# First-step keys loaded whole in the middle, the middle's last stores moved into the attention, filling products ahead of the first 42 half maxima

## What is computed

```python
# layer 0: state space model, then a feed-forward with signs for weights
u  = ssm(layernorm(x))                         # a scan over 2048 steps
y  = clip(layernorm(x) @ sign(W).T * scale + bias)
x1 = x + u + y;  xn = layernorm(x1)
# layer 1, two attentions, 16 heads of 16 features, causal
A  = softmax(q @ k.T / 4 + slope * (j - i)) @ v     # from xn, 16 key heads
B  = softmax(rope(q) @ rope(k).T / 4) @ v           # from rmsnorm(xn), 4 key heads
# then output products, a router, and the two best of 8 experts for each token
```

## Time and profile before

| | us |
|---|---|
| median of three runs | 2366.09 (2365.41 to 2367.84) |
| the profiled execution, its own time | 2358.44 |
| its span, first to last instruction | 2356.0 |
| TensorE busy | 2176.4 (92%) |
| VectorE busy | 2028.9 (86%) |
| ScalarE busy | 1542.3 (65%) |
| GpSimd busy | 671.4 (28%) |
| mean granted clock of TensorE | 0.956 of 2.4 GHz |

### The profile page before, as it was taken

One profiled execution on the slowest core, in us unless ns is written; L12 is line 12 of the kernel. 1 busy time (PEld: TensorE's weight loads), 2 busy tenths in 40 slices (PEclk: granted clock), 3 DMA queues, 4 the chain that ended last, 5 costly groups with the idle time before them and its releaser, 6 DMA issues. The chain is left out here.

```text
span 2356.0 us, 47793 instructions
## 1 busy us (share of the span) xinstructions
PE 2176.4 (92%) x15828; PEld 1282.4 (54%) x15829; DVE 2028.9 (86%) x5148; ACT 1542.3 (65%) x2993; POOL 671.4 (28%) x997
## 2 busy tenths in 40 slices
PE   4599968999999999999999999999998894999997
PEld 2355544444444444444444544544543783888886
DVE  7799858999999999999999999999991664777775
ACT  3144414678888888888888888888888452444443
POOL 5523002232322322322322322322211254333333
PEclk8799977999999999999999999999999886999999
DMA  5179875654554654432432432433222895444443
GB/s 169 58 217 266 276 179 77 119 118 90 103 107 88 108 107 86 92 84 63 92 85 63 92 78 70 92 76 72 69 89 64 292 307 215 78 81 81 82 81 70
DMA packets 176412, 273.23 MB, mean 116 GB/s; under 512 B 53608, under 2 KB 126072, under 8 KB 170372
## 3 DMA queue, kind: packets, MB, share of 16 engines
q0 software_dynamic: 45840, 137.55, 28.6%
q1 hardware_dynamic: 125332, 122.86, 17.3%
q10 hardware_dynamic: 5044, 10.32, 1.5%
HBM read 128.64 MB, written 140.98 MB: 114 GB/s over the span
## 5 line engine op out<-in xcount | busy, mean ns | idle before, releaser
L1524 ACT ACTIVATE a_p<-banks 128x512 f32<-128x512 f32 x2176 | 1131.2, 608 | 256.8 <-PE banks L1417 206.8
L1577 DVE TENSOR_REDUCE a_mx<-banks 128x1 f32<-128x512 f32 x1536 | 943.4, 680 | 20.1 <-PE banks L1406 20.0
L1485 PE MATMUL banks<-a_p,a_v 128*32 128x512 f32 (+3 forms) x5120 | 589.0, 544 | 1.6 <-ACT a_o L1542 1.1
L1406 PE MATMUL banks<-a_k,a_q 52*128 52x512 f32 (+5 forms) x1600 | 446.8, 413 | 1.9 <-DVE a_rowtop L1574 0.3
L1417 PE MATMUL banks<-a_q,a_k 50*128 50x512 f32 (+7 forms) x1600 | 415.8, 396 | 1.1
L1574 DVE CUSTOM_DVE_ANT_0 a_masked<-banks,a_later 128x512 bf16<-128x512 f32 (+3 forms) x768 | 330.8, 484 | 19.2 <-PE banks L1406 17.3
L1417 PEld LDWEIGHTS banks<-a_q,a_k 54*128 54x128 f32 (+1 forms) x1600 | 227.3, 185 | 198.7 <-DVE a_mx L1577 95.6
L1406 PEld LDWEIGHTS banks<-a_k,a_q 52*128 52x128 f32 (+1 forms) x1600 | 224.1, 185 | 118.0 <-DVE a_mx L1577 55.4
L1406 PE MATMUL banks<-a_k,q 48*128 48x512 f32 (+6 forms) x896 | 256.7, 420 | 6.2 <-DMA a_k<-aug_rows 4.6
L1417 PE MATMUL banks<-q,a_k 50*128 50x512 f32 (+7 forms) x896 | 231.5, 402 | 1.1 <-DVE a_orow L1597 0.3
L1485 PEld LDWEIGHTS banks<-a_p,a_v 128*32 128x32 f32 x5120 | 109.3, 108 | 175.0 <-issue 125.3
(11 more groups left out here) (276 smaller groups left out, 2997.2 us busy)
## 6 DMA issues: line engine op xcount, KB each, us to landing
expert_rows<-a_zeros POOLq DMA_DIRECT2D x132, 258.0 KB, 5.3
a_k<-ka_parts POOLq DMA_DIRECT2D x42, 256.0 KB, 6.3
e_x<-expert_rows SPq DMA_DIRECT2D x71, 129.0 KB, 2.3
expert_rows<-e_y SPq DMA_DIRECT2D x71, 128.0 KB
qa_parts<-m_part SPq DMA_DIRECT2D x16, 512.0 KB
ka_parts<-m_part SPq DMA_DIRECT2D x16, 512.0 KB
va_tiles<-m_va SPq DMA_DIRECT2D x8, 1024.0 KB, 6.8
qb_parts<-m_part SPq DMA_DIRECT2D x16, 512.0 KB, 3.8
```

Source lines behind the costliest of these rows:

```text
L1406: ins = pe.matmul(ps[bank][:, col:col + w], q_op[r % 3][part, p, qt * P:(qt + 1) * P], keys_of(r, k0)[part, kp, k0:k0 + w], start=True, st ...
L1485: ins = pe.matmul(ps_o[VW * h:VW * h + VW, c0:c0 + w], v_op[o][:, kt, hk * VW:hk * VW + VW], prob[:, (at + slot) % NPB, col:col + w], star ...
L1524: nc.scalar.activation(prob[:, (t * NSC + n) % NPB, :], ps[bank][:, :], ACT.Exp, scale=SCALE).then_inc(s_ex, 1)
L1577: ins = v.tensor_reduce(top, ps[bank][:, :], AX.X, ALU.max)
```

## The change

- `k0a` (keys of 512 tokens) is gone. `k0`, all 2048 keys of step 0, 16 KB a partition, lies where the first half of `xnT` (the normalised tokens of batch 0) lay, which nobody reads after block 3. POOL loads it in the middle in three groups, the first with the extras, after block 6's second low part, block 6's last, and block 7's second. `first_step_keys`, `keys_of` and the waits on `s_k` are gone.
- The stores of the last `kb` part and of the last `vb` tile are issued by SP first thing in the attention; SP awaits no part or value store at the middle's end, and POOL awaits all of them ahead of the first load of step 1 after half maximum 40.
- `later` and `numbers` are loaded in the front; all engines wait for `s_masks` 80.
- Filling products: 36 instead of 20 at the middle's end; none ahead of the first rows instead of 10; two ahead of each of the first 17 half maxima (`ROWLESS` = 7 + 2 * 5 = 17) and one ahead of each of the next 25 (`WARM` = 42), into the bank just taken.
- Tiles of the attention are allocated in another order.

```diff
             for dst, src in ((M["fill"], "c_fill"),
+                             (M["later"], "c_later"), (M["numbers"], "c_ids"),
...
-def first_keys(eng, M, j):
-    for n in range(NPROD):
...
+def first_keys(eng, M, j, n):
+    at = HALF * j + n * HD
+    eng.dma_start(M["k0"][at:at + HD, :, :].bitcast(F32),
+                  M["ka_d"][PROD_K[n], 0:GH * HD, :].rearrange("(p j d) t -> j d p t", p=PAIRS, j=2)[j]
+                  ).then_inc(M["s_first"], 16)
+
+def first_operands_at(nc, M):
+    at = SBUF_START + F32_BYTES * (P + WIDE + TOK // P + PAIRS * L) + BF16_BYTES * (HALF + 2 * P)
+    M["k0"] = nc.alloc_sbuf_tensor_at("k0", [P, PAIRS, L], F32R, offset=at)
...
+def last_stores(eng, M):
+    eng.dma_start(M["kb_d"][:, (B - 1) * P:B * P, L - BT:L].rearrange("a f t -> f a t"),
+                  M["last_part"][:, :, :].bitcast(F32)).then_inc(M["s_moved"][NBLK - 2], 16)
+    eng.dma_start(M["vb_d"].rearrange("(n p) c -> p n c", p=P)[:, TOK // P - TPB:TOK // P, :],
+                  M["last_values"][:, :, :, :].rearrange("p j h c -> p j (h c)")).then_inc(M["s_moved"][NBLK - 1], 16)
...
@@ middle, POOL @@
-                    for m in range(2):
+                    for m in range(4):
                         pool.wait_ge(s_pst[m], NBB * 16 + 16)
...
-            for j in range(2):
-                first_extras(pool, M, j)
-                first_keys(pool, M, j)
+            for n, rows in enumerate(((NBLK - 2) * NS + 2, (NBLK - 2) * NS + NS, (NBLK - 1) * NS + 2)):
+                pool.wait_ge(s_lo, rows)
+                for j in range(2):
+                    first_keys(pool, M, j, n)
+                    if n == 0:
+                        first_extras(pool, M, j)
...
@@ middle, SP @@
                     sp.wait_ge(s_lo, blk * NS + (m + 1))
+                    if blk == NBLK - 1 and m == NS - 1:
+                        break
...
                 sp.wait_ge(s_va, blk * 2 + 2)
-                sp.dma_start(vb_d[:, blk * TPB:(blk + 1) * TPB, :],
-                             vb[:, :, :, :].rearrange("p j h c -> p j (h c)")).then_inc(s_vst, 16)
-            for m in range(NS):
-                sp.wait_ge(s_pst[m], NBLK * 16 + 16)
+                if blk < NBLK - 1:
+                    sp.dma_start(vb_d[:, blk * TPB:(blk + 1) * TPB, :],
+                                 vb[:, :, :, :].rearrange("p j h c -> p j (h c)")).then_inc(s_vst, 16)
             for i in range(2):
                 sp.wait_ge(s_st[i], NBLK // 2 * 32 + 16)
-            sp.wait_ge(s_vst, NBLK * 32 + 16)
             sp.wait_ge(M["s_first"], NFIRST)
...
-            keep_going(pe, M, ps[0], 20)
+            keep_going(pe, M, ps[0], 36)
...
@@ attention, SP @@
+            last_stores(sp, M)
             for o in range(2):
                 sp.sem_inc(s_os[o], 16)
-            sp.dma_start(later[:, :], A["c_later"]).then_inc(M["s_masks"], 16)
-            first_step_keys(sp, s_k[0], BT, 2 * BT)
...
@@ attention, POOL @@
-            pool.dma_start(numbers[:, :], A["c_ids"]).then_inc(s_zs, 16)
             pool.wait_ge(s_hi, 1)
-            pool.wait_ge(s_zs, 16)
+            pool.wait_ge(M["s_masks"], NMASKS)
...
                     elif t == 0 and what == "max" and n % 5 == 0 and 0 <= n // 5 - 4 < len(LOADS):
+                        if n // 5 == 4:
+                            for done, count in zip(M["s_moved"], M["moved"]):
+                                pool.wait_ge(done, count)
                         pool.wait_ge(s_mt, 2 * n)
                         load(pool, 1, LOADS[n // 5 - 4])
...
@@ attention, PE @@
-                        if t == 0 and n == 2 * KEYED[0]:
-                            pe.wait_ge(s_k[0], NFK)
-                        if t == 0 and n == 2 * KEYED[1]:
-                            pe.wait_ge(s_k[1], NFK)
...
                         take(bank, s_md, t * NMH + (n + 1 + MD0))
+                        if t == 0 and n < WARM:
+                            keep_going(pe, M, ps[bank], 2 if n < ROWLESS else 1)
                         max_half(t + n // NMH, n, bank)
                     elif what == "rows":
-                        if t == 0 and n == 0:
-                            keep_going(pe, M, ps_o, 10)
...
@@ attention, ACT @@
-            first_step_keys(act, s_k[1], 2 * BT, L)
             load(act, 0, ("values", 0, 0))
```

More of the change, by code:

```diff
@@ L13 @@
 ds = bass.ds
+SBUF_START, SBUF_END = 16512, 229344
+F32_BYTES, BF16_BYTES = 4, 2
 P = 128
@@ L156, in _ @@
             sp.dma_start(aug[:, :], A["c_aug"]).then_inc(s_aug, 16)
-            for dst, src in ((M["fill"], "c_fill"),
+            for dst, src in ((M["fill"], "c_fill"), (M["later"], "c_later"), (M["numbers"], "c_ids"),
                              (M["after_q"][0], "c_after0"), (M["after_q"][1], "c_after1")):
@@ L514, in middle @@
         vb_d = M["vb_d"].rearrange("(n p) c -> p n c", p=P)
+        M["last_part"], M["last_values"] = part[NS - 1], vb
         NW = 10
@@ L1105, in attention @@
         ps, ident = M["ps"], M["ident"]
-        q_op = [M["q0"], *(sb(f"a_q{i}", [P, PAIRS, L], F32R) for i in range(1, 3))]
+        sb("a_room_k0", [P, PAIRS, L], F32R)
+        q1 = sb("a_q1", [P, PAIRS, L], F32R)
         v_op = [sb(f"a_v{i}", [P, KT, GH * VW]) for i in range(3)]
@@ L1109, in attention @@
         fill, after_q = M["fill"], M["after_q"]
-        later = sb("a_later", [P, WIDE])
+        later, numbers = M["later"], M["numbers"]
         masked = sb("a_masked", [P, 2, WIDE], BF16)
@@ L1119, in attention @@
         zeros = sb("a_zeros", [P, FILL, DR])
-        numbers = sb("a_numbers", [P, TOK // P])
         raw_w = sb("a_raww", [P, WIDE], F32R)
         high_w = sb("a_highw", [P, WIDE], F32R)
-        k_op = [sb(f"a_k{i}", [P, PAIRS, L], F32R) for i in (0, 2, 1)]
-        k_op = [k_op[0], k_op[2], k_op[1]]
+        q_op = [M["q0"], q1, sb("a_q2", [P, PAIRS, L], F32R)]
+        k2, k1 = sb("a_k2", [P, PAIRS, L], F32R), sb("a_k1", [P, PAIRS, L], F32R)
+        k_op = [M["k0"], k1, k2]
         ps_o = ps[RING]
@@ L1156, in attention @@
         DIRECT = 2
+        NMASKS = 5 * 16
+        WARM, ROWLESS = LEAD, RING + 2 * (LAST_MAX[0] + 1)
         TOPS = NQB - DIRECT
@@ L1232, in load @@
                               va_d[:, ds(b * KT, KT), ds(g * GH * VW, GH * VW)]).then_inc(v_sem, 16)
[L1234 to L1245, removed]
-                              M["aug_d"][SLOPED:2 * SLOPED + 2, j * PAIRS:(j + 1) * PAIRS, lo:hi]).then_inc(done, 16)
         block = ctx.enter_context(nc.Block())
@@ L1386, in mask @@
                 return ins
-            def keys_of(r, k0):
-                return M["k0a"] if r == 0 and k0 < BT else k_op[r % 3]
             holder = {}
@@ L1406, in max_half @@
                     ins = pe.matmul(ps[bank][:, col:col + w], q_op[r % 3][part, p, qt * P:(qt + 1) * P],
-                                    keys_of(r, k0)[part, kp, k0:k0 + w], start=True, stop=True)
+                                    k_op[r % 3][part, kp, k0:k0 + w], start=True, stop=True)
                 ins.then_inc(s_mt, 1)
@@ L1416, in score_half @@
                     kp = 0 if r >= NGB else p
-                    ins = pe.matmul(ps[bank][:, col:col + w], keys_of(r, kt * P)[part, kp, kt * P:(kt + 1) * P],
+                    ins = pe.matmul(ps[bank][:, col:col + w], k_op[r % 3][part, kp, kt * P:(kt + 1) * P],
                                     q_op[r % 3][part, p, qb * QB + c0:qb * QB + c0 + w],
@@ L1603, in _ @@
                 step(t)
-SBUF_END = 229344
-F32_BYTES = 4
 def at_top(nc, M):
@@ L2397, in of_both @@
                 return early.enter_context(nc.sbuf_tensor(name, shape, dt))
-            M["k0a"] = of_both("k0a", [P, PAIRS, BT], F32R)
+            M["later"] = of_both("later", [P, WIDE], F32)
+            M["numbers"] = of_both("numbers", [P, TOK // P], F32)
             M["q0"] = of_both("q0", [P, PAIRS, L], F32R)
```

18 lines of the change are left out of this document (6 added, 12 removed).

## The result

The changed kernel took **2389.88 us** (median of four, 2386.89 to 2392.37) beside 2366.97 for the kernel before (2365.41 to 2368.36): ratio 1.0108, with 95% between 1.0096 and 1.012. It is slower by 1.1%, where 2354.0 was forecast, with a range of 2347 to 2362.

The account below looks back on a forecast made before the run. Bound from 450 us by VectorE and TensorE, so gains come earlier: -7.6 (start) - 4.6 (keys) - 3.8 (ten products) + 3.9 (17 halves) = -12.1, own time 2346.3, median 2354.0 us, range 2347 to 2362.

Parts of the forecast that it names:

- Boundary, gain 7.6 us: Middle to attention: without awaited stores, 36 filling products end at 322.02 and attention starts at 322.35 instead of 329.95.
- Keys, "I take 0": Key loads late in the middle: no cost, 1.4 us of slack at va; bounds no loss and 1.4 us.
- rival 3: Middle ends late: a key load lands after 322 or stores hold va; 1 to 3 us lost, chance 0.09.
- First maxima, 0.683 us a half: 17 halves before rows 0: TensorE needs 0.468 for filling plus 0.215 each, 11.6 us together.
- From rows 0 to the first scores, 4.0 us: Transposes, ScalarE's copy and the rows' DMA: stays 4.0 us, scores at 337.96.
- From scores to rows 1, "I take 0": 23 halves with one filling product each: unchanged from 17.05 us, VectorE the bound; bounds -2 and +12.35.
- rival 1: Scores to rows 1: clock falls at rows 0, filling doesn't raise it; 12.35 us lost, 2366; chance 0.16.
- all at 1.2 GHz, 29.4 us: Upper bound for first scores to rows 1: the whole stretch at half clock, +12.35 us.
- Later, "unchanged, 3 us either way": After rows 1: stall there unchanged; where idle time up to 450 falls may shift, 3 us either way.
- Rival 2: Half clock from the first maxima: 17 halves take 23.2 us, together +11.9, 2378 us; chance 0.06.
- Wrong: rows 1 not before 360: Sign against the forecast, which expected rows 1 turned near 355.
- The granted clock of 1.0 between 322 and 334: Sign for the forecast: full clock from the first maxima up to rows 0, turned near 334.

Follow-up runs that it names:

- e6: e1 with the va and vb stores counted on two semaphores, so each buffer waits only for its own last store: 2348.6 us, ratio 0.9946.
- e5: e1 with the key loads issued right behind the queries', at about 230 us: 2353.97 us, ratio 0.9966.
- e2: The changed kernel with all six key loads at the first of their three points: 2381.11 us, ratio 1.0086 to the kernel before.
- e3: The changed kernel without filling ahead of the half maxima and with all key loads at the first point: 2348.14 us, ratio 0.9951.
- e7: The changed kernel with two filling products ahead of each of the first 17 halves, none ahead of the next 25: 2363.55 us, ratio 1.0017.
- e1: The changed kernel without filling ahead of the first 42 half maxima; the 36 products at the middle's end stay: 2352.02 us, ratio 0.9971.
- e10: e9 with ten filling products in each of two waits for the rows' DMA, at scores 0 and rows 1's scores: 2346.5 us, ratio 0.9951.
- e9: e6 with 26 instead of 36 filling products at the middle's end: 2347.63 us, ratio 0.9954.
- e8: The changed kernel with 60 filling products for 59, all ahead of even halves, so a pair's halves stand together: 2364.73 us, ratio 1.0025.
- the second pair: The kernel before and the changed kernel, both unchanged, run again on another chip: 2359.43 and 2383.23 us.
- e4: The kernel before with the change's filling ahead of its first 42 half maxima, without its ten products ahead of rows 0: 2397.23 us, ratio 1.0161.

## Why the prediction was wrong

**Boundary, gain 7.6 us: the mechanism right, eaten whole by the term put at nothing.** The stores left the middle's path, 36 products took 8.26 us (8.42 forecast), and e6 shows the start forecast. But in the kernel after the last middle product ended 7.3 us late, and the boundary took 0.75 us instead of 0.33. Of the 7.6 nothing was left. The other two gains of the sum did come: TensorE no longer waits for keys (4.6 us) nor spends the ten products (3.8), and is busy for all of the 18.11 us from the first filling to rows 0.

**Keys, "I take 0", the first step that failed.** The slack at `va` was found rightly (1.4 us) and so was the consumer; rival 3 names it, with 1 to 3 us for what became 7.5. The size was wrong: 1.4 to 2 us of delay stood in the bounds, and the store came 10.3 us later. I had priced the added bytes at the full rate. Together with the stores the loads are dearer than that. The view of the DMA queues in 299 to 315 us, of the kernel before:

```profile
DMA packets 3660, 5.36 MB, mean 335 GB/s; under 512 B 150, under 2 KB 1686, under 8 KB 3659
...
q1 hardware_dynamic: 3659, 5.35, 106.6%
```

and of the kernel after, run again:

```profile
DMA packets 2788, 4.37 MB, mean 273 GB/s; under 512 B 164, under 2 KB 1665, under 8 KB 2659
...
q1 hardware_dynamic: 2595, 3.31, 71.9%
q0 software_dynamic: 192, 1.05, 33.6%
```

The columns are packets, MB and share of the 16 engines' time. Both are full, and 1 MB less goes through (5.36 and 4.37). SyncE's queue (q1) spends 1.066 x 16 us / 5.35 = 3.2 us of all engines per MB before and 3.5 after; POOL's (q0) spends 5.1. So POOL's 1.05 MB cost what 1.6 MB of stores cost. What makes them dear (the 16 partitions, the queue, the layout of the source) was not varied. The queue also did not begin empty: `va` of block 6, issued before 299, took 16.3 us, and from 283 on the first group of loads had raised the engines' share from 0.67 to 0.95. A backlog of stores with 1.4 us of slack behind it isn't priced by the rate of the added bytes alone. The Trainium skill, "DMA: Bandwidth & Descriptors", section on queues, rings and completion order, has each engine take turns between queues; the direction agrees, but the estimate of about 2 us made from it was five times too small. That e5 moves the wait, e2 and e3 shorten it to 5.71 and 3.84 us, and e6 removes it with the landing still late, shows both halves of this cause.

The way from that wait to TensorE had its own slack, which neither the prediction nor its rival counted. VectorE waited 9.31, 8.62 and 7.22 us in the kernel after, in the same run again and in e7, and TensorE behind it 4.74, 4.05 and 2.65: about 4.6 us were covered. On the other side the wait had a price of its own. In the kernel after the four products behind it took 3.59 us, at a mean granted clock of 0.71 from 315 to 320.88; after e7's shorter wait they took 1.99:

```profile
314.30 1.99 PE L683 MATMUL banks<-m_hT,m_wb 128*128 128x512 f32 x4 [2.65 <-DVE m_va L963]
```

So 4.74 us of waiting and 1.6 us of slower products make up 6.3 of the 7.3.

**First maxima, 0.683 us a half: the second step that failed.** Measured 1.06. I had taken 0.215 us, the minimum of the earlier trace rows, for 512 columns. The groups of the kernel before with the shapes kept apart show whose minimum it is:

```profile
L1406 PE MATMUL banks<-a_k,a_q 52*128 52x512 f32 x560 | 190.0, 461 | 1.0 <-DVE a_rowtop L1574 0.3
...
L1406 PE MATMUL banks<-a_k,a_q 52*128 52x128 f32 x80 | 17.3, 219 | 0.0
```

The short form takes 0.219; a 512-column half 0.461, 0.42 from start to start. The 0.279 of the earlier trace rows by busy time is right only because busy time counts two halves that run together once. "Nothing overlaps between two whole-array products" was in the text, and was used to pick the smaller number, when it means that the pair loses its overlap. The full price is 2 x 0.229 (8.26 / 36) + 0.42 + about 0.18 that remains of the 0.64, near one weight load of that line (184 ns at the median; that it is this load was not tried). By this sum 17 halves are 18.0 us, measured 18.1, 6.5 over the forecast of 11.6. Rows 0 came 14.0 us later than forecast (348.00, 333.96): 7.5 by the start, 6.5 by this.

**From rows 0 to the first scores, 4.0 us: right** (4.03).

**From scores to rows 1, "I take 0", the third and dearest: 39.09 us instead of 17.05.** Two things in one. The clock did what rival 1 said: the last two windows of the kernel after show it high up to the stall (1.00 until 353) and low for the 57.5 us behind it (0.50), with one filling product ahead of each of the 23 halves. But even the bound "all at 1.2 GHz, 29.4 us" was 9.7 us too low, since it doubled the busy time of overlapping halves (9.3 us) and put the filling at 0.234 each. In fact 23 x 1.45 = 33.4 us go to halves with their filling alone. e1 and e7 show the other side: without the filling the same stretch, at 0.59 and 0.50 of the clock, takes 17.4 and 18.0 us. VectorE was the bound and its cover was larger than I gave it, until filling used it up. Why single filling products did not raise the clock again is not settled by these runs: in the earlier trace rows ten in a row ended in 2.4 GHz, and so did e10's (the 512-column score behind them took 0.49 us, in e9 0.80), e8's pairs did not reach it either, and no run varied the share alone.

**Later, "unchanged, 3 us either way".** It held for the change itself in the second pair (0.5 us) and not in the first (5.2), and it was too narrow for kernels that reach rows 1 early. Windows from rows 1 to the last store of step 0, of the kernel before, of e6 and of e10:

```profile
367.13:481.61 114.48, 102.38 (x670) 50.10 (x674) 100.56 (x264) 66.35 (x126) 30.18 (x55) 0.87 0.60 104
```

```profile
351.88:475.21 123.33, 114.74 (x670) 54.54 (x674) 101.25 (x264) 66.19 (x126) 30.13 (x55) 0.74 0.56 95
```

```profile
352.13:469.50 117.37, 107.04 (x690) 51.97 (x694) 100.15 (x264) 66.14 (x126) 30.14 (x55) 0.88 0.62 101
```

e6 is 15.3 us ahead at rows 1 and gives 8.9 of it back, with a clock of 0.74 instead of 0.87. If the time at 1.2 GHz is worked out from the mean clock, this stretch grows over all profiles by about 0.25 us for each us of it, within 1.6 us; e9 and e10 lie over 3 us above that line (e10 in the last fence, 2.9 us longer than before at an even higher clock), and this part stays open. In medians e6 is about 12 us ahead.

**The sum.** Forecast own time 2346.3, measured 2388.86, 42.6 over: 7.5 for the start, 6.5 for the first halves, 22.0 for the second, 5.2 after rows 1 (which the second pair does not repeat), 1.3 elsewhere. The forecast's sign hung on the filling. Rival 2 ends on the right side (2378) by the wrong mechanism: the clock was at 2.4 when the maxima began. The rival that held was not among them: TensorE becomes the bound at any clock in the first stretch, because filling breaks the pairs. "Wrong: rows 1 not before 360" was the sign that came true; rival 3, "the middle ends late", came true beside it, at more than twice its size. The granted clock of 1.0 between 322 and 334, one of the signs of being right, came true too and helped nothing.

## What to carry to other kernels

Before filling products go between matmuls, see whether the matmuls run in pairs in the profile (starts together, or a group's busy time over its count below the duration of one): filling of the whole array between the two doubles their cost (0.44 us became 0.84 here), so put it ahead of the pair, or where TensorE waits anyway. Price a matmul by its own shape, never by a group's minimum. And a transfer moved to where nothing seems to need the queue is not free when the DMA engines are full: count engine time per byte of that pattern and the slack behind every store in flight, and give each buffer's store its own semaphore, so that a late store holds only its own buffer.

## What the hardware showed unexpectedly

- Loads of 256 KB into 16 partitions on POOL's queue took 5.1 us of all 16 engines' time per MB (299 to 315 us; kernel after, run again) beside 3.2 to 3.5 for SyncE's stores; the total rate fell from 335 to 273 GB/s at the same share.
- TensorE worked 74.18 of 74.99 us in e4 at a mean granted clock of 0.50. Being busy with short matmuls and filling in turn did not bring 2.4 GHz.
- The block boundary cost TensorE 0.75 us in the kernel after (both runs), e1, e3, e5 and e6, against 0.33 in the earlier trace rows; where the difference comes from was not tried. In e2, e7, e8, e9 and e10 it was 1.03 to 1.10 us, and there TensorE started 0.92 us behind VectorE's last operation of the middle each time.
